# Gathered rows and heads' outputs turned by transposing DMAs on SP's queue instead of by TensorE and ScalarE

## The chip, the cores and the metric

The kernel runs on one core of a Trainium2 chip. Its time is the device time of one execution in microseconds; lower is better. Engines are called as in the profile: PE (TensorE), DVE (VectorE), ACT (ScalarE), POOL (GpSimd) and SP (SyncE, which here only issues DMAs).

## The reference

Eight sequences of 1024 tokens with 512 features are normalised to xn. The result is x plus a Mamba-2 block of xn plus a routed attention of xn. The change concerns the attention. In it, each of 4 groups ranks the tokens by router logits, takes 512 of them as queries and 256 as keys and values, and attends with 8 heads of 64 features:

```python
q_top, q_idx = jax.lax.top_k(jnp.einsum('bnd,gd->bgn', x, w_qr), 512)
queries = x[bidx, q_idx]
kv_top, kv_idx = jax.lax.top_k(jnp.einsum('bnd,gd->bgn', x, w_kvr), 256)
key_values = x[bidx, kv_idx]
q = jnp.einsum('bgnd,ged->bgne', queries, w_q)
k, v = jnp.split(jnp.einsum('bgnd,ged->bgne', key_values, w_kv), 2, axis=-1)
# heads; v *= sigmoid(kv_top); one null key and value in front
attn = jax.nn.softmax(jnp.einsum('bghid,bghjd->bghij', q, k) * DH ** -0.5, axis=-1)
o = jnp.einsum('bghij,bghjd->bghid', attn, v)            # heads side by side: (b, g, 512, 512)
o = jnp.einsum('bgne,gde->bgnd', o, w_out) * jax.nn.sigmoid(q_top)[..., None]
# scatter-add to the tokens, mean over how often each was taken, null token where never
```

## The kernel before, in words

The first half of the program (to about 1856 us) is the Mamba block; it also writes every normalised token to DRAM (`rows`) as two half-precision parts, high and low, so that products come close to single precision (three matmuls for each: high by high, high by low, low by high). The second half is the attention, 32 items (4 groups by 8 sequences). An item n is made of steps:

- DVE finds the tokens' places from their ranks (`rank`, L1803, from `rbc`, which SP loads in two parts, `rank_load`, L2417) and writes them as indices (`slot`). POOL gathers six blocks of 128 rows by indirect DMAs into `gat[0]` to `gat[5]` (`gather`, L2270): four of queries, two of keys.
- `row(n, j)`: a block has one token per partition, but the projections need features on partitions. PE turns the 8 squares of 128 x 128 of a block into a PSUM bank (L1332), ACT copies them to `xq` (queries) or `xk` (keys) (L2116).
- PE projects: `q` (L1345, 4 steps of 12 matmuls), `k` (L1360, 2), `v` (L1374, 2). ACT takes the high part of each, DVE the low part. SP copies halves of `ka` (`keys`, L2423) and `qa` to `qb` (`q_again`, L2429).
- `max` (L1390, 16 steps) and a reduction give each query's maximum; this shift is turned and SP puts it into `qb` (`shift_in`, L2435). The scores (L1420, L1421) wait for it.
- For each of 8 heads: `score` on PE, exponential to `pf` (L2153) and high part to `ph` (L2159) on ACT, low parts on DVE (L1901) and POOL (L2297), `value` on PE (L1437 to L1441), the division on DVE (L1910), then `o_high` on ACT (L2164) and `o_low` on POOL (L2302), which fill `ohl`, the outputs of all heads.
- `oturn(n, qt)`: PE turns the 8 squares of one block of 128 queries from `ohl` (L1449), ACT copies them to `oT[qt]` (L2171).
- `out(n, qt)`: 12 matmuls (L1460) give the output block; ACT scales it (`res`, L2178), POOL adds it to the result in DRAM by an indirect DMA (`store`, L2291).

The items overlap: while the heads of item n run, PE also prepares item n + 1, and turns and projects the outputs of item n - 1. What stands where is decided when the program is built: `make_plan` mixes PE's steps by shares (`Part(feed, start, end)`), and an `Order` then plays all engines through with a duration for each step and lays every engine's instructions down in the order in which they would start. `add(engine, us, step, after, seats, extra)` gives a step its duration, what it comes after, its PSUM banks, and `extra`, how long after its end its result lands. On the chip each engine works its list off in order; semaphores make it wait. `Queue.wait_ge` leaves out a wait that an earlier one covers.

The Mamba block already has two kinds of transposing DMAs on SP: `turn` (L2346, tile `xhT` from `xh`, 128 x 1024 halves) and `gate` (L2352, `yT` from `yhl`, 128 x 2048).

Of the kernel before, what the change touches and what calls it, by code (L numbers as in the profile page):

```python
# [12 lines left out]
P = 128  # L13
# [36 lines left out]
NSLOT = 4  # L50
NW = 4 * D
# [313 lines left out]
def chain(*gens):  # L365
# [10 lines left out]
    "row": [("single", 1, 1.2)],  # L376
# [8 lines left out]
    "oturn": [("single", 1, 1.4)],  # L385
# [5 lines left out]
    "row": [(0.6, "row_out")],  # L391
# [8 lines left out]
    "oturn": [(0.6, "oturn_out")],  # L400
# [9 lines left out]
    "row": lambda n, j: (("gather", n, j), 4.0),  # L410
# [5 lines left out]
    "oturn": lambda n, qt: (("o_low", n, H - 1), 0.8),  # L416
    "out": lambda n, qt: (("oturn_out", n, qt), 0.6),
# [20 lines left out]
def arrange(plan, line):  # L438

    first = [("x_in", 0)]  # L440
    alone = Order(plan.twin(), first, ahead=AHEAD_M)
    arrange_steps(alone, [step for step in line if step[0] not in ("rank_in", "slots", "row")], False)
    alone.run()
    order = Order(plan, first, [t for step, t in alone.at.items() if alone.nodes[step][0] == "DVE"], ("bit", "ranks", "ranks_zero"), ahead=AHEAD_M)
    arrange_steps(order, line, True)
    order.run()


def arrange_steps(order, line, late):
# [13 lines left out]
    for step in line:  # L463
# [26 lines left out]
        elif name == "row":  # L490
            add("PE", 0.45, step, [("gather", 0, b)], [("single", [("row_out", 0, b)])])
# [118 lines left out]
    for j in range(RT):  # L610
        add("POOL", 1.05, ("gather", 0, j), [("slot", 0)], extra=3.0)
        add("ACT", 0.6, ("row_out", 0, j), [("row", 0, j), ("z", NCH - 1, 1)])


def arrange_items(plan, line):

    done = [("weight_low", 0, k) for k in range(FIRST_SLICES)] + [("nulls", 0), ("slot", 0)]
    for j in range(RT):
        done += [(name, 0, j) for name in ("rank", "gather", "row", "row_out")]
# [15 lines left out]
    def back_by(name, n, h, k):  # L635
# [3 lines left out]
    seats = {"q": "q_low", "k": "k_low", "v": "v_low", "row": "row_out", "max": "max_out", "shift_turn": "shift_out",  # L639
             "null_turn": "null_out", "score": "soft", "value": "norm_o", "oturn": "oturn_out", "out": "res"}  # L640
    takes = {"q": 2.6, "k": 2.62, "v": 2.6, "row": 0.45, "max": 0.23, "shift_turn": 0.24, "null_turn": 0.24,
             "score": 0.88, "value": 0.95, "oturn": 0.45, "out": 2.6}
    for step in line:
        name, n, k = (*step, 0)[:3]
        if name == "row":
            after = [("gather", n, k)]
        elif name in "qkv":
            after = each("row_out", n, QT if name == "q" else RT) + [("weight_low", n // NB, NSP // 4 * ("qkv".index(name) + 1) - 1)]
# [10 lines left out]
        elif name == "oturn":  # L659
            after = [("o_low", n, H - 1)]  # L660
        else:
            after = [("oturn_out", n, k), ("weight_low", n // NB, NSP - 1)]
# [12 lines left out]
    for n in range(ITEMS):  # L675
        if n:
# [13 lines left out]
        for e in range(KT):  # L690
            add("ACT", 1.2, ("k_out", n, e), [("k", n, e), two] + ([("keys_id", 1)] if n == 1 else []))
            add("DVE", 1.4, ("k_low", n, e), [("k_out", n, e)])
            add("ACT", 0.7, ("v_out", n, e), [("v", n, e), ("row_out", n, RT - 1), ("value", n - 2, H - 1)])
# [15 lines left out]
        for h in range(H):  # L709
# [16 lines left out]
def make_plan():  # L726
# [68 lines left out]
    for j in range(RT):  # L795
        record.append(("row", 0, j))
# [3 lines left out]

    def turn_rows(n):
        for j in range(RT):
            yield ("row", n, j)
            yield 0.43
# [37 lines left out]
    def turn_out(n):  # L842
        for qt in range(QT):
            yield ("oturn", n, qt)
            yield 0.43

# [9 lines left out]
    for gen in (prepare(0), maxima(0), turn_rows(1)):  # L856
        Feed(gen, 1, record).to(1)
    for n in range(ITEMS):
        others = []
        if n:  # L860
            others.append(Part(Feed(turn_out(n - 1), QT * 0.43, record), -2.9, 6.0))
# [1648 lines left out]
```

## Time and profile before

| | |
|---|---|
| median of 3 runs | 3683.78 us (3683.2 to 3689.54) |
| the profiled execution, its own time | 3691.88 us |
| its span, first to last instruction | 3690.6 us |
| PE busy | 3470.4 us, 94% |
| DVE, ACT, POOL busy | 2934.9 (80%), 2445.5 (66%), 1871.1 (51%) |
| granted PE clock, mean | 0.98 |
| DMA packets | 498362, 344.43 MB |

The page cuts the span into 40 slices of 92 us. A digit is the busy share in tenths, PEclk the granted clock, DMA the share of the 16 DMA engines; the attention begins in slice 21:

```profile
PE   6899999999999999999669999999999999999998
DVE  6898988989898988989968767777767777677764
ACT  5767776677676676776346666676666766666665
POOL 1332423333333433333348788776566766566565
PEclk9899999999999999999879999999999999999999
DMA  5454454455454444544374344354333434334333
```

A line of the list of groups reads: line, engine, operation, written tile <- read tiles (buffer numbers left out; `pair` is PSUM, `id` the identity matrix of a transpose), shapes, count | busy us, mean ns of one | idle time of the engine just before, and what ended it. SPq is the queue of DMAs that SP issues; the duration of such a row is the time that SP takes to issue, and "landing" the time from issue until the data have arrived.

### The profile page before, as it was taken

The page shows a single profiled execution, that of the slowest core. Times are in us where ns is not written, and L with a number is a line of the kernel's source. Part 1 is how long each engine was busy: PE and PEld are TensorE (multiplying, and loading weights), DVE is VectorE, ACT ScalarE, POOL GpSimd, SP SyncE. Part 2 cuts the span into 40 slices and gives each one's busy share as a digit, 9 for nine tenths or more (in the row PEclk, how much of TensorE's full clock was granted, in tenths as well). Part 3 has the DMA queues.
Part 4 walks back from the last instruction along what each step waited for, and adds up shares of the span by engine and source line. Part 5 has one row for each costly group of instructions (what it writes and reads, how often), then busy time and mean ns, then how long its engine had stood idle before and what let it go on. Part 6 is the DMA issues. An engine that isn't in the chain of part 4 may idle for free.

```text
span 3690.6 us, 69594 instructions
## 1 busy us (share of the span) xinstructions
PE 3470.4 (94%) x26872; PEld 2075.7 (56%) x26872; DVE 2934.9 (80%) x5336; ACT 2445.5 (66%) x4649; POOL 1871.1 (51%) x1483
## 2 busy tenths in 40 slices
PE   6899999999999999999669999999999999999998
PEld 4455555555555555555335656656666566666665
DVE  6898988989898988989968767777767777677764
ACT  5767776677676676776346666676666766666665
POOL 1332423333333433333348788776566766566565
PEclk9899999999999999999879999999999999999999
DMA  5454454455454444544374344354333434334333
GB/s 158 98 110 109 114 103 86 101 124 121 113 120 92 107 102 109 116 101 92 67 123 84 74 74 80 72 112 86 69 74 80 105 73 83 71 72 83 70 68 39
DMA packets 498362, 344.43 MB, mean 93 GB/s; under 512 B 239368, under 2 KB 422792, under 8 KB 495985
## 3 DMA queue, kind: packets, MB, share of 16 engines
q1 hardware_dynamic: 441712, 237.05, 28.1%
q0 software_dynamic: 56320, 102.94, 16.3%
q8 instruction: 213, 3.49, 0.4%
q14 instruction: 117, 0.95, 0.1%
HBM read 176.19 MB, written 101.71 MB: 75 GB/s over the span
## 4 chain that ended last, share of the span: by engine, by line
PE 69%; DVE 14%; DMA 4%; issue 4%; ACT 3%; POOL 1%; another core or an unknown queue 0%; DVEq 0%; ACTq 0%
PE pair L1345 8%; PE pair L1297 7%; PE pair L1219 7%; PE pair L1460 6%; PE pair L1267 6%; PE pair L1360 4%; PE pair L1307 4%; PE pair L1374 4%; PE pair L1421 3%; PE pair L1420 3%; PE pair L1390 2%; PE pair L1278 2%; PE pair L1287 2%; PE pair L1441 2%; PE pair L1332 2%
## 5 line engine op out<-in xcount | busy, mean ns | idle before, releaser
L2297 POOL TENSOR_TENSOR ph<-pf,ph 128x512 f16<-128x512 f32 x256 | 380.0, 1486 | 317.7 <-ACT ph L2159 314.7
L1610 DVE SCALAR_TENSOR_TENSOR cv<-raw,taps,cv 128x512 f32<-128x512 f32 x480 | 429.0, 921 | 27.8 <-ACT cv L2018 26.5
L1866 DVE TENSOR_REDUCE smx<-pair 128x2 f32<-128x514 f32 x512 | 350.3, 686 | 79.7 <-PE pair L1390 76.5
L1219 PE MATMUL pair<-xhT,whi 128*128 128x512 f16 x1280 | 385.4, 383 | 8.0 <-ACT btok L2038 2.1
L1297 PE MATMUL pair<-ohi,yT 128*128 128x512 f16 x1024 | 322.5, 387 | 39.1 <-DMA yT<-yhl 38.3
L1267 PE MATMUL pair<-zhi,xhT 128*128 128x512 f16 x1024 | 329.8, 384 | 8.5 <-ACT btok L2038 7.5
L2153 ACT ACTIVATE pf<-pair 128x1024 f32<-128x1024 f32 x256 | 262.1, 1024 | 92.3 <-PE pair L1421 88.3
L1901 DVE TENSOR_TENSOR ph<-pf,ph 128x512 f16<-128x512 f32 x256 | 232.0, 907 | 99.7 <-ACT ph L2159 97.4
L2048 ACT ACTIVATE de<-de,cum 128x128 f32<-128x128 f32 x1024 | 309.4, 388 | 1.2
L2159 ACT CAST ph<-pf 128x1024 f16<-128x1024 f32 x256 | 267.9, 1047 | 4.5
L1828 DVE SCALAR_TENSOR_TENSOR qa<-pair,qa 64x512 f16<-64x512 f32 x256 | 176.6, 690 | 92.1 <-ACT qa L2124 88.4
L1307 PEld LDWEIGHTS pair<-xdt,de 128*128 128x128 f32 x2048 | 239.7, 193 | 16.7 <-issue 8.7
L2302 POOL TENSOR_TENSOR ohl<-of,ohl 128x256 f16<-128x256 f32 x256 | 202.2, 799 | 85.8 <-ACT ohl L2164 83.7
L1219 PE MATMUL pair<-xhT,wlo 128*128 128x512 f16 x640 | 244.5, 382 | 0.0
L1307 PE MATMUL pair<-xdt,de 128*128 128x64 f32 x2048 | 237.7, 275 | 3.8 <-DVE dxs L1646 3.8
L2291 POOL DMA_INDIRECT y<-res,slot_i x128 | 213.5, 1668 | 51.6 <-ACT res L2178 31.9
L1441 PE MATMUL pair<-vhi,ph 128*128 128x65 f16 x2048 | 238.4, 194 | 0.0
L1439 PE MATMUL pair<-vhi,ph 128*128 128x65 f16 x2048 | 238.4, 194 | 0.0
L1440 PE MATMUL pair<-vlo,ph 128*128 128x64 f16 x2048 | 237.9, 193 | 0.0
L2231 POOL TENSOR_TENSOR yn<-yn,neghalf 128x1 f32<-128x1 f32 x64 | 48.7, 760 | 350.3 <-DVE yn L1700 350.1
L2270 POOL DMA_INDIRECT gat<-rows,slot_i x192 | 194.0, 1010 | 58.6 <-issue 29.0
L1219 PEld LDWEIGHTS pair<-xhT,whi 128*128 128x128 f16 x1280 | 123.8, 99 | 168.9 <-issue 35.2
(267 smaller groups left out, 10300.2 us busy)
## 6 DMA issues: line engine op xcount, KB each, us to landing
de<-cum SPq DMA_DIRECT2D x64, 1024.0 KB, 9.4
rows<-rowt SPq DMA_DIRECT2D x16, 1040.0 KB, 6.6
xin<-x SPq DMA_DIRECT2D x16, 1024.0 KB, 8.7
y<-xin SPq DMA_DIRECT2D x16, 1024.0 KB, 5.9
y<-ob POOLq DMA_DIRECT2D x64, 256.0 KB, 4.5
qb<-qa SPq DMA_DIRECT2D x32, 512.0 KB
rbc<-rank SPq DMA_DIRECT2D x63, 256.0 KB
wst<-wkv SPq DMA_DIRECT2D x32, 256.0 KB
```

The lines of the kernel that those rows point to most:

```text
L1219: ins = pe.matmul(bk[:], w[:, k, ws], xt[:, ha, k, :], start=n == 0, stop=n == 3 * KD - 1)
L1267: pe.matmul(pz[:], xt[:, ha, k, cs], w[:, k, j * 512:(j + 1) * 512], start=n == 0, stop=False)
L1297: ins = pe.matmul(bk[:], yT[:, ha * KI + k, :], w[:, k, :], start=k == 0 and n == 0, stop=k == KI - 1 and n == 2)
L1307: ins = pe.matmul(pw[:, h * HD:(h + 1) * HD], de[ch % 2][:, h, :], xdt[:, h, :], start=True, stop=True)
L1345: ins = pe.matmul(bk[:], w[:, k, ws], xq[:, ha * KD + k, :], start=n_ == 0, stop=n_ == 3 * KD - 1)
L1441: ins = pe.matmul(o, p_[:, 1, j, qs_], vhi[u][:, j, h, :], start=False, stop=j == KT - 1, skip_group_check=True)
L1610: ve.scalar_tensor_tensor(c_[:], r_[:, t:t + BLK], taps[:, ct, t:t + 1], c_[:], ALU.mult, ALU.add).then_inc(done, 1)
L1866: ve.tensor_reduce(smx[:, qt, 2 * h2:2 * h2 + 2], sc[:, :, 0:NK + 1], AX.X, ALU.max)
L2048: ins = ac.activation(d_[:, h, :], d_[:, h, :], ACT.Relu, bias=cum_t[i % 2][:, c, h:h + 1], scale=-1.0)
L2153: ac.activation(f[:].rearrange("p k q -> p (k q)"), bank("score", n, h)[:], ACT.Exp, scale=SCALE).then_inc(S.pf, 1)
L2159: ac.copy(p_[:, 0], f[:]).then_inc(S.ph, 1)
L2297: po.tensor_tensor(p_[:, 1, 1], f[:, 1], p_[:, 0, 1], ALU.subtract).then_inc(S.plp, 1)
```

## The change

The two kinds of transposes leave PE and their copies leave ACT. SP issues them as transposing DMAs from SBUF to SBUF: one for each gathered block (six an item, `row`), and one for two blocks of outputs (two an item, `oturn(n, a)`). For the latter `ohl` is laid out as query block, high or low, feature, and `oT` becomes two tiles of two blocks. The PSUM seats of both kinds disappear. POOL's next gather into `gat[j]` now waits until all turns of its kind (queries or keys) have landed, ACT's first cast of the next item into `ohl` until both output turns have landed. The scale of v from the gathered keys stays on DVE as a step of its own, `row_score`. The planner gets durations for the new steps, and the shares by which PE's steps are mixed are set anew; some tiles change places in SBUF.

```diff
+ROW_ISSUE, ROW_LANDS = 0.6, 4.0
+O_ISSUE, O_LANDS = 0.6, 5.0
...
-    "out": lambda n, qt: (("oturn_out", n, qt), 0.6),
+    "out": lambda n, qt: (("oturn", n, qt // 2), 4.0),
...
-                add("POOL", 1.05, ("gather", n, j), [("slot", n), ("row", n - 1, j), ("row_out", n - 1, j)], extra=4.0)
-                add("ACT", 0.6, ("row_out", n, j), [("row", n, j), ("q", n - 1, KD - 1) if j < QT else ("v_low", n - 1, KT - 1)])
+                add("POOL", 1.05, ("gather", n, j), [("slot", n), ("row", n - 1, RT - 1 if j >= QT else QT - 1)] + ([("row_score", n - 1, j)] if j >= QT else []), extra=4.0)
+                read = ("q", n - 1, KD - 1) if j < QT else ("v", n - 1, KT - 1)
+                add("SP", ROW_ISSUE, ("row", n, j), [("gather", n, j), read], extra=ROW_LANDS)
...
-            add("ACT", 0.42, ("o_high", n, h), [("norm_o", n, h)] + each("oturn", n - 1, QT))
+            add("ACT", 0.42, ("o_high", n, h), [("norm_o", n, h)] + each("oturn", n - 1, QT // 2))
...
-            add("ACT", 0.6, ("oturn_out", n, qt), [("oturn", n, qt), ("out", n - 1, qt)])
+            if qt % 2 == 0:
+                add("SP", O_ISSUE, ("oturn", n, qt // 2), [("o_low", n, H - 1), ("out", n - 1, qt + 1)], extra=O_LANDS)
...
-    for gen in (prepare(0), maxima(0), turn_rows(1)):
+    for gen in (prepare(0), maxima(0)):
...
-            others.append(Part(Feed(turn_out(n - 1), QT * 0.43, record), -2.9, 6.0))
...
-            others.append(Part(Feed(maxima(n + 1), 10.2, record), -0.6, 1.1))
+            others.append(Part(Feed(maxima(n + 1), 10.2, record), -0.7, 1.1))
...
-            others.append(Part(Feed(finish(n - 1), 10.4, record), -1.0, 1.0))
-        if n + 2 < ITEMS:
-            others.append(Part(Feed(turn_rows(n + 2), RT * 0.43, record), -1.9, 1.25))
+            others.append(Part(Feed(finish(n - 1), 10.4, record), -0.7, 1.2))
...
-            def row(n, j):
-                g16 = gat[j][:].bitcast(F16)
-                q.wait_ge(S.gat[j], 16 * (n + 1))
-                wait_given_back(q, "row", n, j)
-                b16 = bank("row", n, j)[:].bitcast(F16)
-                for c in range(2 * KD):
-                    ins = pe.transpose(b16[:, c * P:(c + 1) * P], g16[:, c * P:(c + 1) * P], id16[:])
-                ins.then_inc(S.gt_mm, 1)
...
             def norm_o(n, h):
                 q.wait_ge(S.of, H * n + h + 1)
-                q.wait_ge(S.oT_mm, QT * n)
-                ac.copy(ohl[:, 0, :, h * DH:(h + 1) * DH], of[h % 2][:]).then_inc(S.oh, 1)
...
+                for a in range(2):
+                    q.wait_ge(S.oT[a], 16 * n)
+                ac.copy(ohl[:, :, 0, h * DH:(h + 1) * DH], of[h % 2][:]).then_inc(S.oh, 1)
...
             def gather(n, j):
                 q.wait_ge(S.slot, n + 1)
-                q.wait_ge(S.gt_mm, RT * (n - 1) + j + 1)
+                q.wait_ge(S.xr[j // QT], 16 * (KT if j // QT else QT) * n)
...
+            def row(n, j):
+                q.wait_ge(S.gat[j], 16 * (n + 1))
+                if n == 0:
+                    q.wait_ge(S.z_mm, 2 * NCH)
+                    q.wait_ge(S.xs, NCT * NBLK)
+                if j < QT:
+                    q.wait_ge(S.q_mm, KD * n)
+                else:
+                    q.wait_ge(S.k_mm, KT * n)
+                    q.wait_ge(S.v_mm, KT * n)
+                dst, s0 = (xq, j) if j < QT else (xk, j - QT)
+                sp.dma_start_transpose(dst[:, :, s0 * P:(s0 + 1) * P], gat[j][:].bitcast(F16)[:, 0:2 * D]).then_inc(S.xr[j // QT], 16)
...
+            def oturn(n, a):
+                q.wait_ge(S.olo, H * (n + 1))
+                q.wait_ge(S.out_mm, QT * (n - 1) + 2 * a + 2)
+                sp.dma_start_transpose(oT[a][:], ohl[:, 2 * a:2 * a + 2].rearrange("p q h d -> p (q h d)")).then_inc(S.oT[a], 16)
```

SP's instructions for one item in the middle of attention, before. `rbc` is the load of ranks, `qb<-shT` the shift that the scores wait for, `qb<-qa` and `ka<-ka` the copies within one item; in brackets the semaphores that SP waits for.

```order
L2435 DMA qb1<-shT 8x8x512 [waits shiftT]
L2429 DMA qb0<-qa0 64x4096 [waits score_mm,q_high]
L2423 DMA ka0<-ka0 64x8x256 [waits k_high]
L2417 DMA rbc<-rank 128x1024 [waits ranked,slot]
L2417 DMA rbc<-rank 128x1024 [waits ranked]
```

The same stretch after the change, from one output turn to the copy of ka (the second `rbc` follows it):

```order
L2394 DMA_TRANSPOSE oT0<-ohl 128x16x128 [waits out_mm,o_low]
L2371 DMA_TRANSPOSE xq<-gat0 128x8x128 [waits q_mm,gat_in0]
L2394 DMA_TRANSPOSE oT1<-ohl 128x16x128 [waits out_mm]
L2371 DMA_TRANSPOSE xq<-gat1 128x8x128 [waits gat_in1]
L2358 DMA rbc<-rank 128x1024 [waits ranked]
L2371 DMA_TRANSPOSE xq<-gat2 128x8x128 [waits gat_in2]
L2371 DMA_TRANSPOSE xq<-gat3 128x8x128 [waits gat_in3]
L2371 DMA_TRANSPOSE xk<-gat4 128x8x128 [waits v_mm,k_mm,gat_in4]
L2371 DMA_TRANSPOSE xk<-gat5 128x8x128 [waits gat_in5]
L2389 DMA qb1<-shT 8x8x512 [waits shiftT]
L2383 DMA qb0<-qa0 64x4096 [waits score_mm,q_high]
L2377 DMA ka0<-ka0 64x8x256 [waits k_high]
```

The eight turns have moved in between the copies: the second output turn stands behind the first row turn, and the shift behind all six.

ACT's instructions around the turned outputs, before: `vhi` is the high part of v, `oT` the copies of turned outputs, `ohl<-of` the cast of a head's output, `res` the scaling of an output block.

```order
L2140 ACTIVATE vhi<-pair,kscore 128x8x64 [waits row_score,v_mm]
L2171 COPY oT<-pair 128x512 [waits o_turned] x3
L2164 CAST ohl<-of 128x4x64 [waits o_turned,o_head]
L2171 COPY oT<-pair 128x512
L2140 ACTIVATE vhi<-pair,kscore 128x8x64 [waits v_mm]
L2153 ACTIVATE pf<-pair 128x1024 [waits p_low_p,p_low_v,score_mm]
```

After:

```order
L2087 ACTIVATE vhi<-pair,kscore 128x8x64 [waits row_score,v_mm]
L2087 ACTIVATE vhi<-pair,kscore 128x8x64 [waits v_mm]
L2100 ACTIVATE pf<-pair 128x1024 [waits p_low_p,p_low_v,score_mm]
L2106 CAST ph<-pf 128x1024 [waits value_mm,p]
L2119 ACTIVATE res<-pair,qsc 128x512 [waits score_in0,res_out0,out_mm]
L2112 CAST ohl<-of 128x4x64 [waits oT1,oT0,o_head]
```

The first cast of the next item now stands behind the softmax step and behind the `res` of the first output block, and waits for both turns.

## Rows read from the trace of the kernel before

**Rows 1.** Stretches: length, PE, PEld, DVE, ACT, POOL busy (instructions), PEclk, DMA share, GB/s.
```profile
1900.00:2300.00 400.00, 373.13 (x3689) 233.70 (x3689) 302.36 (x681) 256.49 (x391) 322.33 (x270) 0.98 0.43 86
...
2386.80:3599.00 1212.20, 1186.14 (x11891) 747.92 (x11889) 881.65 (x2031) 809.34 (x1223) 781.19 (x688) 1.00 0.40 80
```

**Rows 2.** Waits of PE, 1900 to 3650 us: total us, times, longest.
```profile
PE pair L1437 <- ACT xq L2116: 6.9, 20, 0.8
```

**Rows 3.** Groups of instructions by line: busy us, mean ns, idle before.
```profile
L1332 PE MATMUL pair<-id,gat 128*128 128x128 f16 x1536 | 111.0, 223 | 32.9 <-DMA gat<-rows,slot_i 24.1 <-DVE snl L1867 4.6 <-ACT res L2178 1.8
...
L1449 PE MATMUL pair<-id,ohl 128*128 128x128 f16 x1024 | 68.9, 222 | 2.3 <-POOL ohl L2302 2.3
```

**Rows 4.** The chain of waits, 2600 to 2640 us: start, length, what.
```profile
2609.53 0.89 PE pair L1449 x16
...
2616.95 2.59 PE pair L1460 x12
...
2624.75 0.89 PE pair L1332 x16
...
2633.87 4.36 DMA gat<-rows,slot_i
```

**Rows 5.** Stretch of attention, ACT line 2116 alone, then ACT line 2171 alone.
```profile
1860.00:3690.00 1830.00, 108.90 (x192) 0.99 0.41 80
...
1860.00:3690.00 1830.00, 71.43 (x128) 0.99 0.41 80
```

**Rows 6.** Timeline of SP's queue: start, duration, instruction.
```profile
2639.25 0.76 SPq L2435 DMA_DIRECT2D qb<-shT  x1
...
2660.31 0.61 SPq L2423 DMA_DIRECT2D ka<-ka  x1
...
2715.85 0.61 SPq L2423 DMA_DIRECT2D ka<-ka  x1
```

**Rows 7.** Tiles xhT, then yT: issue in ns min/median/max; landing.
```profile
L2346 SPq DMA_TRANSPOSE xhT<-xh x64: 1232/1291/6160, 32.3 to 1610.4; - x64
...
DMA to landing us min/median/max: 2.7/3.8/10.6
...
L2352 SPq DMA_TRANSPOSE yT<-yhl x64: 1322/1888/3949, 132.1 to 1834.1; - x64
...
DMA to landing us min/median/max: 4.2/4.3/10.4
```

**Rows 8.** Stretches behind a yT turn issued at 1567.73: PEclk, DMA share, GB/s.
```profile
1568.70:1569.70 1.00, 1.00 0.82 162
1569.70:1570.70 1.00, 1.00 1.16 215
1570.70:1571.70 1.00, 1.00 0.79 148
```

**Rows 9.** Timeline of PE where attention begins.
```profile
1869.36 5.45 PE L1332 MATMUL pair<-id,gat 128*128 128x128 f16 x48 [22.19 <-DMA gat<-rows,slot_i]
...
1874.60 0.71 PE L1345 MATMUL pair<-xq,wqhi 128*128 128x512 f16 x2
```

**Rows 10.** Stretches there: PE busy, PEclk, DMA share, GB/s.
```profile
1873.00:1874.00 1.00, 1.00 (x12) 0.50 0.85 243
...
1875.00:1876.00 1.00, 1.00 (x6) 1.00 0.02 4
```

**Rows 11.** Timeline of PE at the last item's end.
```profile
3669.93 3.59 PE L1449 MATMUL pair<-id,ohl 128*128 128x128 f16 x32 [2.31 <-POOL ohl L2302]
...
3673.32 0.54 PE L1460 MATMUL pair<-whi,oT 128*128 128x512 f16 x1
```

**Rows 12.** Timeline of one item, from its last head to its output matmuls.
```profile
2605.04 0.38 PE L1420 MATMUL pair<-qa,ka 128*128 128x512 f16 x1
...
2606.27 0.96 POOL L2270 DMA_INDIRECT gat<-rows,slot_i  x1 [0.33 <-DVE slot_i L1813]
2607.51 0.67 POOL L2302 TENSOR_TENSOR ohl<-of,ohl 128x256 f16<-128x256 f32 x1 [0.28 <-ACT ohl L2164]
```

More of the change, by code:

```diff
@@ L441, in arrange @@
     alone = Order(plan.twin(), first, ahead=AHEAD_M)
-    arrange_steps(alone, [step for step in line if step[0] not in ("rank_in", "slots", "row")], False)
+    arrange_steps(alone, [step for step in line if step[0] not in ("rank_in", "slots")], False)
     alone.run()
@@ L611, in arrange_steps @@
         add("POOL", 1.05, ("gather", 0, j), [("slot", 0)], extra=3.0)
-        add("ACT", 0.6, ("row_out", 0, j), [("row", 0, j), ("z", NCH - 1, 1)])
+        add("SP", ROW_ISSUE, ("row", 0, j), [("gather", 0, j), ("z", NCH - 1, 1)], extra=ROW_LANDS)
+        if j >= QT:
+            add("DVE", 0.1, ("row_score", 0, j), [("gather", 0, j)])
 def arrange_items(plan, line):
@@ L618, in arrange_items @@
     for j in range(RT):
-        done += [(name, 0, j) for name in ("rank", "gather", "row", "row_out")]
+        done += [(name, 0, j) for name in ("rank", "gather", "row")]
+        if j >= QT:
+            done.append(("row_score", 0, j))
     order = Order(plan, done, keep=KEEP, ahead=AHEAD)
@@ L637, in back_by @@
         return (name, *divmod(H * n + h - k, H))
[L639 to L642, printed above, removed]
+    seats = {"q": "q_low", "k": "k_low", "v": "v_low", "max": "max_out", "shift_turn": "shift_out",
+             "null_turn": "null_out", "score": "soft", "value": "norm_o", "out": "res"}
+    takes = {"q": 2.6, "k": 2.62, "v": 2.6, "max": 0.23, "shift_turn": 0.24, "null_turn": 0.24,
+             "score": 0.88, "value": 0.95, "out": 2.6}
     for step in line:
         name, n, k = (*step, 0)[:3]
[L645 to L648, printed above, removed]
+        if name in "qkv":
+            after = each("row", n, QT if name == "q" else RT) + [("weight_low", n // NB, NSP // 4 * ("qkv".index(name) + 1) - 1)]
         elif name == "max":
@@ L799, in make_plan @@
     plan.append(("mamba_done",))
[L801 to L804, printed above, removed]
     def prepare(n):
@@ L1045, in program @@
         qb = [sb(ctx, "qb0", [P, H, NQ], F16)]
-        oT.append(sb(ctx, "oT2", [P, 2 * KD, P], F16))
+        res = [sb(ctx, "res0", [P, D], F32)]
         gat = sb2(ctx, "gat", [P, ROW], F32, RT)
@@ L1064, in program @@
         null_bc = sb(ctx, "null_bc", [P, D], F32)
-        res = [sb(ctx, "res0", [P, D], F32)]
+        res.append(sb(ctx, "res1", [P, D], F32))
         smx = sb(ctx, "smx", [P, QT, H], F32)
@@ L1442, in value @@
                 ins.then_inc(S.pv, 1)
-            def oturn(n, qt):
-                q.wait_ge(S.olo, H * (n + 1))
-                wait_given_back(q, "oturn", n, qt)
-                b16 = bank("oturn", n, qt)[:].bitcast(F16)
-                for j in range(2 * KD):
-                    ins = pe.transpose(b16[:, j * P:(j + 1) * P], ohl[:, j // KD, qt, (j % KD) * P:(j % KD + 1) * P], id16[:])
-                ins.then_inc(S.oT_mm, 1)
             def out_(n, qt):
@@ L2185, in scalar_engine @@
                     "attention": attention, "weight_high": weight, "table": table_, "keys_id": keys_id,
-                    "row_out": row, "q_out": qs, "k_out": ks, "v_out": vs, "null_p": null_p,
-                    "soft": score, "high_p": high_p, "o_high": norm_o, "oturn_out": oturn, "res": out_}
+                    "q_out": qs, "k_out": ks, "v_out": vs, "null_p": null_p,
+                    "soft": score, "high_p": high_p, "o_high": norm_o, "res": out_}
             for step in plan:
```

90 lines of the change are left out of this document (26 added, 64 removed).

## The prediction

> **What bounds the kernel now.** I read the stretches of the attention stage first, then PE's waits, then the chain of waits through one item, and single timelines where a number was wanted. The change touches attention alone, the second half of the span. In its middle PE is busy 1186.14 of 1212.20 us at full granted clock, DVE 881.65, ACT 809.34, POOL 781.19 [rows 1]: 97.9% against at most 73%. SP issues the same instruction of neighbouring items, the copy inside ka, at 2660.31 and 2715.85 [rows 6]; 22 items fill the stretch, 55 us each, of which PE stands 1.2. Of what it stands, one kind is 6.9 us in 20 pieces and ends with ACT's copies to xq [rows 2], so even that hangs on work that goes. PE's own queue is the bound: what leaves it shortens the span one for one, unless the new route makes PE wait.
>
> **What is removed, and how to size it.** By the groups of lines, the transposes of gathered rows keep PE busy 111.0 us and those of the heads' outputs 68.9 us [rows 3], 179.9 together. That is too much: busy time of a line alone counts the tail of its last matmul, in which the next step's matmuls already run. The chain shows what a step really occupies: 16 transposes, two steps, take 0.89 us for either kind [rows 4], 0.445 us for a step of 8. There are 32 x 6 + 32 x 4 = 320 steps. 310 of them lie inside the run: 310 x 0.445 = -138 us, 4.45 per item of 55. The other ten are the first item's six and the last item's four; they run at the low clock and come below. ACT also loses 108.90 + 71.43 us of copies [rows 5]; it is 67% busy and PE covers all of it, so by itself it is worth nothing. If another engine were the bound, it would be a gain, no cost.
>
> **What is added: per item six turns of rows and two of outputs, all on SP.** The stage before attention has both instructions. The turn of 128 x 1024 halves (256 KB, one gathered block) holds SP 1.29 us and lands after 3.8; the turn of 128 x 2048 (512 KB, two blocks of outputs) holds it 1.89 us and lands after 4.3; the worst landed after 10.6 and 10.4 [rows 7]. SP is held 6 x 1.29 + 2 x 1.89 = 11.5 us more per item of 50; it issues little now, so the queue has room. What matters is what stands behind a waiting turn.
> On the DMA engines, a lone 512 KB turn takes shares of 0.82, 1.16 and 0.79 in three stretches of 1 us [rows 8]: 2.8 us of all sixteen; half of that, 1.4, for 256 KB. Per item 6 x 1.4 + 2 x 2.8 = 14 us, beside 0.40 x 55 = 22 us of today [rows 1]: 36 of 50.5 us, a share of 0.71. That is busy, not full, and landings may grow. The Trainium skill ("Advanced Engine Details and Errata", section X-Bar Transpose (TRN2)) says that transposing DMAs are as fast as regular ones, 350 to 400 GB/s expected; by that, 512 KB take an estimated 1.4 us and the share would be 0.57. The trace does not agree: the lone turn moved at most 215 GB/s in a stretch [rows 8]. I go by the row.
>
> **Outputs.** In the item shown the last head leaves PE at 2605.04 and its low half is made by 2607.51 + 0.67 = 2608.18 [rows 12]; then 4.3 to land, 2612.5. Meanwhile PE has, in the new order, a score, half of v and a head's values (today these end at 2609.53, 4.4 us after 2605.04 [rows 4, 12]), then the other half of v (12 wide matmuls, 2.59 us as in [rows 4]), another score, another head's values and two maxima (4.4 - 2.6 = 1.8, and about 0.4): 9.2 us, until 2614.2. The turn is in time by 1.7 us. ACT's first cast into ohl for the next item now waits for both output turns. The second stands behind a row turn that waits for a gather issued at 2606.27 [rows 12]; a gather takes 4.36 from issue to use [rows 4]: 2610.6, then 1.3 for the row turn's issue and 4.3 to land, 2616.2. In ACT's new order a res stands before that cast, which waits for the first output matmuls, 2614.2 + 2.6 = 2616.8. So this wait is covered by the other.
> **Rows.** The last row turn of an item waits for the last gather, issued at 2633.87 and there 4.36 us later, 2638.2 [rows 4]; with 1.3 us of issue, SP would come to the copy of the shift (qb<-shT) at 2639.5, and it does so at 2639.25 today [rows 6]. Nothing is lost; q and k of the turned rows begin later than that.
> **New waits, in between.** By medians none of the three shows, with margins of 0.6 to 1.7 us against landings that scatter up to 6 us above their median [rows 7]. I take 0.25 us per item, +8 us (bounds 0 and 31 x 6.1 = 189, every output turn at the worst landing). Against it stand waits that go with the steps: 6.9 us [rows 2], and before the row turns 32.9 - 22.2 = 10.7 us [rows 3, 9]. I take half of these 17.6, -9 us (bounds -18 and 0).
>
> **Start.** PE turns from 1869.36 and begins q at 1874.60 [rows 9]. Now SP issues four turns from 1869.4, the last at 1869.4 + 3 x 1.29 = 1873.2, landed at 1877.0: q is 2.4 us later. PE has stood 22.19 us by then [rows 9], and its granted clock is 0.50 (1.2 GHz) while it turns, 1.00 (2.4 GHz) from 1875 on [rows 10]. The turns took the slow stretch, 5.2 us; now q's matmuls do, at half speed, +2.6. Together +5.0.
> **End.** The last outputs are turned from 3669.93, the output matmuls begin at 3673.32 [rows 11], 3.4 us; a DMA takes 4.3, +0.9, and PE comes back from standing, +2.6 by the same reckoning. +3.5.
>
> **Sum.** -138 + 8 - 9 + 5.0 + 3.5 = -130.5 us. The profiled execution took 3691.9 us (its span 3690.6): 3561.4. The median of the runs, 3683.8, is 8.1 us below it: 3553.
>
> **Rivals.**
> A (10%), the full busy time counts and waits vanish: -179.9 for all 320 steps, with 5.0 + 5.2 and 3.5 + 3.4 given back at the ends: -163, 3521 (3510 to 3530). For it: the groups' busy time [rows 3]. Against it: 0.89 us for 16 in the chain [rows 4].
> B (17%), turns hidden in part: the landings grow with the DMA share from 0.40 to 0.71 by 3 us, 1.3 us more than the outputs' margin, and the ACT cast is late as well; 1.3 to 3 us per item, +40 to +93: 3593 to 3646. For it: single landings of 10 us. Against it: the medians are from shares of 0.4 to 0.5 too.
> C (5%), slower: SP issues the second output turn behind the row turn that waits for gather 0. If gathers, under the added traffic, take 9 us more than 4.36, that turn lands at 2625 and ACT stands at its ohl cast for 8.5 us; scores are not drained and PE stands. 31 x 8.5 = 263 us: 3816. It decides from 130.5 / 31 = 4.2 us per item on. Against it: gathers are spread over 28 us of the item, and ordinary ones go between the turns' packets. The Trainium skill ("VectorE: DVE Perf Modes", sections The three transpose paths and Rules for kernel authors) is on the side of B and C: TensorE turns 128 x 128 in 390 ns, the DMA crossbar in 1309, and TensorE is to be used where PSUM will do. For one turn the trace agrees (3.8 us to land 8 blocks [rows 7], 0.445 on PE [rows 4]); the rule prices latency, and here PE's time is what is short.
> D (4%), POOL bounds the first items, where it also makes weights: busy 322.33 of 400 us [rows 1], 87% if 7 items lose 4.45 us each. If it gives back half of them, +16: 3569, inside my range.
> E (2%), waits of 4 us per item eat it all: no change.
>
> **How the numbers follow.** My forecast, 3535 to 3585, 62%. The range, 3520 to 3600, adds D, most of A and the lower edge of B. About 0.2%, 7 us, is what a measurement of this kernel can tell from no change: faster 0.93, same 0.02, slower 0.05.
>
> **What would show each step.** Items of about 51 us at SP's copy of ka; PE's share in the middle of attention still 97% or more; no wait of PE for DMA xq or xk after the first item, and little for oT; row turns landing in about 4 us, output turns in 4.3 to 5; a DMA share of 0.7; q 2.4 us later behind the first gathers, at the low clock. I am wrong if one of PE's waits for a turn passes 1 us per item, or if ACT stands at its first ohl cast.

## The result: 34 us faster, where 130 were forecast

| | before | changed | |
|---|---|---|---|
| median of the runs, us | 3683.8 | 3649.4 | ratio 0.990, 95% interval 0.988 to 0.992 |
| profiled execution, us | 3691.9 | 3642.1 | its span: 3690.6, 3640.7 |

The change makes the kernel 1.0% faster; 3553 us was forecast, from 3520 to 3600. The profiled executions are 49.8 us apart; the sum, made between profiled executions, was 130.5. So 81 us are missing (96 by the medians, which are 34 us apart; the profiled execution of the changed kernel is the fastest of its four). The page of the changed kernel (its span in 40 equal slices, and SP's queue with its packets, MB and share of the 16 DMA engines):

```profile
PE   6899999999999999999748999999999999999997
...
PEclk9899999999999999999868999999999999999998
DMA  5444544465554445444387576777676676577664
...
q1 hardware_dynamic: 777584, 320.97, 42.5%
```

The DMA row holds 6 and 7 where it held 3 and 4; this came as forecast (0.71). The stretches of attention show what did not. First the changed kernel, then the kernel before over the same long stretch (columns as in [rows 1]):

```profile
1900.00:2300.00 400.00, 358.49 (x3163) 207.25 (x3164) 303.96 (x678) 220.96 (x320) 318.96 (x267) 0.94 0.70 131
...
1900.00:3500.00 1600.00, 1501.40 (x13602) 881.71 (x13603) 1235.54 (x2767) 932.96 (x1356) 1109.29 (x983) 0.97 0.70 132
```

```profile
1900.00:3500.00 1600.00, 1546.15 (x15427) 973.20 (x15428) 1178.24 (x2691) 1057.61 (x1602) 1107.31 (x959) 1.00 0.41 82
```

PE stands for 1600 - 1501.4 = 98.6 us where it stood for 53.9, and its granted clock is 0.97 where it was 1.00. Summed over the 80 stretches of 20 us in it (20 us times 1 less the clock), the clock takes 43.0 us; before, 6.8. So 45 us went into idle time of PE and 36 into its clock, 81 together, about what is missing. This is an account of one stretch and not an exact sum: a low clock while PE stands costs nothing but is counted in the 36, and the first and last items lie outside the stretch.

Single items show the same. An item is taken from one copy inside ka on SP to the next. The first row below is an item of the kernel before; the second is an item of the changed kernel without a long wait, the third one with waits:

```profile
3381.10:3435.70 54.60, 54.12 (x545) 34.16 (x544) 39.16 (x93) 35.68 (x53) 34.18 (x31) 1.00 0.38 75
```

```profile
3286.10:3335.90 49.80, 49.39 (x466) 29.74 (x465) 39.42 (x92) 29.84 (x44) 31.89 (x30) 1.00 0.70 132
3069.60:3129.90 60.30, 55.07 (x466) 31.02 (x464) 41.96 (x99) 30.49 (x43) 32.97 (x32) 0.92 0.62 120
```

With the same 466 matmuls an item takes 49.8 or 60.3 us. In the good one PE's work is 4.73 us less than before (forecast 4.45); five items have 49.8, while the mean of the 31 distances between these copies is (3544.76 - 1887.00) / 31 = 53.5, before 55.1. Of the 10.5 us between the two, 5.7 are more busy time for the same matmuls, at a mean clock of 0.92. The loss is not spread evenly: the first seven distances sum to 379.6 us and before to 375.8, no gain at all, where 31 us was forecast; the other 24 are 53 us shorter, of 107.

What begins the bad item is in its chain of waits (start, length, what):

```profile
3071.48 0.68 POOL ohl L2243
3072.17 7.88 DMA oT<-ohl
3080.05 0.05 issue
3080.10 4.45 PE pair L1421 x12
...
3085.22 2.59 PE pair L1421 x12
3087.81 0.22 PE pair L1359 x2
```

The last half of ohl is written at 3072.16, the turn is issued at once and lands 7.9 us later, not 4.3. PE has done what the order put in between and stands 1.8 us. The 12 output matmuls behind it take 4.45 us, and 2.59 a little later: the wait cost 1.8 us and the clock as much again. Stretches of 2 us show the clock:

```profile
3076.00:3078.00 2.00, 2.00 (x34) 1.46 (x33) 1.86 (x5) 1.47 (x2) 0.00 (x0) 1.00 1.26 263
3078.00:3080.00 2.00, 0.27 (x9) 0.15 (x5) 1.97 (x6) 1.28 (x2) 0.60 (x1) 1.00 0.52 197
3080.00:3082.00 2.00, 1.90 (x5) 0.73 (x6) 1.90 (x3) 0.00 (x0) 0.55 (x1) 0.54 0.88 162
3082.00:3084.00 2.00, 2.00 (x7) 0.74 (x6) 0.00 (x0) 0.00 (x0) 0.00 (x0) 0.61 1.14 211
3084.00:3086.00 2.00, 2.00 (x14) 1.20 (x13) 1.19 (x3) 0.98 (x2) 0.45 (x1) 1.00 0.80 151
```

The DMA engines are full in the 2 us before PE stands (share 1.26), not while it stands (0.52). In the two stretches behind the idle time the clock is 0.54 and 0.61, near the lower level (1.2 GHz). The Trainium skill ("TensorE: Matmul & The Clock Gate", Part 1) says that the chip sets this clock by how busy TensorE has been of late; the rows agree.

SP's timeline of this item has the queue that the prediction spoke of: the second output turn is issued 8.2 us after the first, behind the row turn that the prediction expected to wait for its gather.

```profile
3072.17 3.65 SPq L2394 DMA_TRANSPOSE oT<-ohl  x1
3079.10 1.24 SPq L2371 DMA_TRANSPOSE xq<-gat  x1
3080.39 1.81 SPq L2394 DMA_TRANSPOSE oT<-ohl  x1
```

PE's longest waits of the changed kernel from 1900 to 3540 us, and one of ACT's from 1900 to 3550 (total us, times, longest):

```profile
PE pair L1421 <- DMA oT<-ohl: 16.1, 11, 3.8
PE pair L1359 <- DVE snl L1827: 13.8, 17, 2.8
PE pair L1359 <- DVE of L1870: 8.9, 5, 2.2
PE pair L1367 <- DVE shift L1832: 7.6, 2, 5.3
```

```profile
ACT ohl L2112 <- DMA oT<-ohl: 40.7, 26, 4.3
```

Only the first names a DMA. The next three are steps of the maxima, which wait for VectorE: for reductions and the shift made of them (`snl`, `shift`), and for the division of a head's output (`of`). The kernel before already had waits of this kind, and [rows 2] shows only the fourth line of its list. The three above it, 1900 to 3650 us, were as large or larger and belong to steps that stay:

```profile
PE pair L1406 <- DVE pnm L1890: 10.5, 8, 2.9
PE pair L1390 <- DVE snl L1867: 9.0, 11, 2.1
PE pair L1420 <- DVE snl L1867: 7.9, 6, 1.8
```

ACT's stand at its ohl cast is what I had named as a sign of being wrong. From this reading I held the output turns guilty, with the clock that their waits take; the first experiments test that.

### The profile page after: what moved, and what is told of

It reads as the page before. It is cut to its first block, busy times and chain, and to the rows that moved or that the text cites. A ratio compares the mean times of both kernels' runs of the same rounds, so it can differ in the third digit from the quotient of the medians.

```text
span 3640.7 us, 64398 instructions
## 1 busy us (share of the span) xinstructions
PE 3360.3 (92%) x24312; PEld 1940.5 (53%) x24312; DVE 2962.7 (81%) x5336; ACT 2273.6 (62%) x4329; POOL 1850.6 (51%) x1483
## 4 chain that ended last, share of the span: by engine, by line
PE 58%; DVE 14%; DMA 8%; issue 5%; POOL 5%; ACT 4%; SPq 1%; another core or an unknown queue 0%; POOLq 0%; ACTq 0%; DVEq 0%
PE pair L1314 7%; PE pair L1275 7%; PE pair L1197 7%; PE pair L1421 7%; PE pair L1245 6%; PE pair L1285 4%; PE pair L1329 3%; DMA oT<-ohl 2%; PE pair L1343 2%; PE pair L1389 2%; PE pair L1390 2%; PE pair L1359 2%; PE pair L1256 2%; PE pair L1265 2%; DMA de<-cum 2%
## 5 line engine op out<-in xcount | busy, mean ns | idle before, releaser
L2238 POOL TENSOR_TENSOR ph<-pf,ph 128x512 f16<-128x512 f32 x256 | 354.8, 1386 | 243.8 <-ACT ph L2106 241.6
L1861 DVE TENSOR_TENSOR ph<-pf,ph 128x512 f16<-128x512 f32 x256 | 254.8, 995 | 84.3 <-ACT ph L2106 81.3
L1285 PEld LDWEIGHTS pair<-xdt,de 128*128 128x128 f32 x2048 | 244.7, 196 | 20.4 <-issue 12.5
L1408 PE MATMUL pair<-vhi,ph 128*128 128x65 f16 x2048 | 243.8, 196 | 0.5 <-issue 0.5
L1410 PE MATMUL pair<-vhi,ph 128*128 128x65 f16 x2048 | 243.7, 195 | 0.3 <-issue 0.3
L1406 PE MATMUL pair<-nvb,pnT 96*128 96x65 f16 x1024 | 202.3, 198 | 21.3 <-issue 6.7
```

The costliest lines, as they stand in the source:

```text
L1285: ins = pe.matmul(pw[:, h * HD:(h + 1) * HD], de[ch % 2][:, h, :], xdt[:, h, :], start=True, stop=True)
L2238: po.tensor_tensor(p_[:, 1, 1], f[:, 1], p_[:, 0, 1], ALU.subtract).then_inc(S.plp, 1)
```

## The experiments

Medians in us; each ratio is to the kernel before, run beside it on the same chip. The median of the kernel before was 3681 to 3691 there, so kernels that did not run beside each other are compared by their ratios (0.001 is 3.7 us). An interval of a ratio is some 8 us to either side. PE idle, the sum of the clock's loss (as above) and the DMA share are of the 1600 us from 1900 on in the profiled execution. Each kernel named _weave has an order of its own, described below, so a difference between two of them also holds how well each order came out.

| kernel | median | ratio (95%) | PE idle | clock | DMA |
|---|---|---|---|---|---|
| before | 3684 | 1 | 54 | 7 | 0.41 |
| changed | 3649.4 | 0.990 (0.988 to 0.992) | 99 | 43 | 0.70 |
| rows_only | 3690.5 | 1.000 (0.999 to 1.002) | 99 | 40 | 0.58 |
| outs_only | 3648.6 | 0.988 (0.986 to 0.991) | 58 | 16 | 0.52 |
| planner_costs | 3643.2 | 0.987 (0.984 to 0.989) | 98 | 46 | 0.70 |
| before_weave | 3656.7 | 0.993 (0.990 to 0.995) | 28 | 6 | 0.41 |
| outs_weave | 3597.3 | 0.976 (0.974 to 0.978) | 21 | 7 | 0.54 |
| rows_weave | 3631.3 | 0.987 (0.984 to 0.990) | 59 | 19 | 0.62 |
| both_weave | 3620.2 | 0.984 (0.981 to 0.987) | 87 | 39 | 0.74 |
| keys_weave | 3611.0 | 0.979 (0.977 to 0.981) | 40 | 10 | 0.60 |
| outs_shadow | 3631.9 | 0.984 (0.981 to 0.986) | 42 | 17 | 0.71 |
| outs_small | 3605.0 | 0.979 (0.977 to 0.981) | 23 | 8 | 0.56 |
| outs_stall | 3782.0 | 1.025 (1.022 to 1.027) | 120 | 75 | 0.49 |

### One half of the change at a time

rows_only puts the outputs' steps back on TensorE and ScalarE, outs_only the rows'. The core of each edit to the changed kernel:

```diff
 rows_only, TensorE:
+            def oturn(n, qt):
+                q.wait_ge(S.olo, H * (n + 1))
+                wait_given_back(q, "oturn", n, qt)
+                ... ins = pe.transpose(b16[:, j * P:(j + 1) * P], ohl[:, qt, j // KD, ...], id16[:])
 outs_only, TensorE:
+            def row(n, j):
+                q.wait_ge(S.gat[j], 16 * (n + 1))
+                wait_given_back(q, "row", n, j)
+                ... ins = pe.transpose(b16[:, c * P:(c + 1) * P], g16[:, c * P:(c + 1) * P], id16[:])
```

> Only the gathered rows are turned by transposing DMAs (192 of them); the heads' outputs go back to TensorE and ScalarE (128 steps), with the weave of the kernel before for them. Theory: what ate the forecast gain is the output turns alone: they land some 7 us after their issue in the loaded queue, PE waits for oT, and the short idle times lower the granted clock. Then this kernel removes 192 x 0.445 = 85 us of PE and pays nearly nothing: 3600 to 3620 us, below the changed kernel (3649), clock 0.99 and over from 1900 to 3540, DMA share about 0.57. Rival 1 (every transposing DMA costs in proportion to its bytes, through a loaded DMA side: slower gathers, clock, DVE): a gain in proportion, 0.6 x 34 us, so about 3664 us. Rival 2 (the written order is what costs, not the transfers): PE idles in front of the max and score steps as this planner's order has it, 3640 or more, with no wait for a DMA among the first.

Measured: 3690.5, no gain. My theory is wrong as it stood: the row turns alone take 85 us of work off PE and give nothing. It came out as rival 2 had it. PE idle and clock lose as much as in the changed kernel, 99 and 40 us.

> Only the heads' outputs are turned by transposing DMAs (64 of them, 512 KB each); the rows are turned on TensorE and ScalarE as before. Theory: output turns are the cost: 128 x 0.445 = 57 us of PE removed, some 25 us of waits for oT and some 20 us of clock given back: 3665 to 3690 us, with oT still landing over 6 us after its issue and the clock below 0.99. Rival 1 (load in proportion to bytes): 3670 us too, but with oT landing in about 5 us, since the rows' turns are gone from the queue, and waits for oT under 10 us. If the turns cost only what was forecast (landing 4.3 us): 3630 us.

Measured: 3648.6, as much as the whole change, and better than the theory and rival 1 had it. PE waits 5.1 us for oT. The output turns are not the guilty half: alone they gain as much as both kinds together.

planner_costs tells the planner what the trace shows, which alters the order of instructions only:

```diff
-ROW_ISSUE, ROW_LANDS = 0.6, 4.0
-O_ISSUE, O_LANDS = 0.6, 5.0
+ROW_ISSUE, ROW_LANDS = 1.3, 4.0
+O_ISSUE, O_LANDS = 3.0, 4.5
```

> The changed kernel with the planner told what its trace shows: a row turn takes SP 1.3 us and lands 4.0 us later, an output turn takes SP 3.0 us and lands 4.5 us later (before 0.6 + 4.0 and 0.6 + 5.0). Only the order of the instructions changes. Theory: PE's waits for oT (22.7 us) shrink, since out comes later in the order, and a part of the clock comes back: 3615 to 3640 us. Rival (the loss is contention and does not hang on order): within 5 us of 3649.

Measured: 3643.2, its interval overlaps the changed kernel's. The theory's detail came true and its sum did not: PE waits 0.4 us for oT, and stands as long as before. PE's first waits are now in the maxima:

```profile
PE pair L1359 <- DVE snl L1827: 20.5, 32, 2.4
PE pair L1359 <- ACT pf L2100: 12.9, 15, 0.9
...
PE pair L1421 <- DMA oT<-ohl: 0.4, 1, 0.4
```

rows_only has the same picture, without one DMA among its first waits:

```profile
PE pair L1388 <- DVE pnm L1871: 22.4, 16, 3.2
PE pair L1372 <- DVE snl L1848: 19.3, 30, 2.7
PE pair L1372 <- ACT pf L2121: 16.3, 29, 0.9
PE pair L1402 <- DVE snl L1848: 14.2, 18, 2.9
```

New theory O: the turns were filler, short work that PE had while the maxima waited. A maxima step gives PE 0.22 us of matmuls (the last row of the chain above) for a pair of banks that VectorE then reduces in two pieces, 512 in all; by the groups of the changed kernel (busy us, mean ns):

```profile
L1826 DVE TENSOR_REDUCE smx<-pair 128x2 f32<-128x514 f32 x512 | 349.7, 684 | 88.3 <-PE pair L1359 85.5 <-issue 2.0
```

0.22 us on PE, 2 x 0.68 on VectorE. By the theory the turns stood in between; take them out, and PE stands there, unless other work is put in.

### The order set anew, with and without turns

In four kernels the shares between which the weave spreads each kind of step were chosen again. both_weave against the changed kernel (with planner_costs' lines, and 6.0 us for a gather's landing in place of 4.0):

```diff
-KEEP = 4.0
-AHEAD, AHEAD_M = 12, 4
+KEEP = 8.0
+AHEAD, AHEAD_M = 16, 4
-            others.append(Part(Feed(prepare(n + 1), 20.8, record), 0.2, 2.0))
-            others.append(Part(Feed(maxima(n + 1), 10.2, record), -0.7, 1.1))
+            others.append(Part(Feed(prepare(n + 1), 20.8, record), -0.2, 1.9))
+            others.append(Part(Feed(maxima(n + 1), 10.2, record), -0.6, 1.0))
-            others.append(Part(Feed(finish(n - 1), 10.4, record), -0.7, 1.2))
+            others.append(Part(Feed(finish(n - 1), 10.4, record), -1.1, 1.8))
```

> The control: the kernel before, no turn moved, only its weave set anew in the same way (prepare 0.1 to 1.8, maxima -0.5 to 1.1, finish -1.1 to 1.9, row turns -2.5 to 1.75, output turns -1.9 to 7.2). Its PE was busy for 97 to 99% of each stretch. Theory O: at most 0.5% faster, 3670 to 3690 us, so that what the other three win belongs to the turns. If it gains 1% or more, the new order is worth its gain without any transposing DMA and the moved turns are worth less than the comparison says.

The control, 3656.7, more than I expected of it: the order alone is worth 0.7%, so the others are compared with it. Its PE stands 28 us of 1600 instead of 54.

> Outputs by transposing DMAs, rows on TensorE (as outs_only, 3648.6 us), with the measured costs of an output turn and the weave set anew (prepare 0.0 to 2.1, maxima -0.9 to 1.1, finish -1.5 to 2.0, row turns -1.5 to 1.55). Its PE was idle for 58.5 us of 1640, near the 54.4 us of the kernel before, so theory O and rival D both leave little to win: 3630 to 3650 us.

3597.3, far below what I expected, 59.4 us under the control (128 x 0.445 = 57; the difference is known to some 11 us), and the fastest kernel here. PE stands 21 us of 1600:

```profile
1900.00:3500.00 1600.00, 1578.58 (x15464) 983.38 (x15463) 1278.05 (x2825) 1042.71 (x1576) 1131.51 (x1007) 1.00 0.54 104
```

> Rows by transposing DMAs, outputs on TensorE (as rows_only, 3690.5 us, the time of the kernel before), with the weave set anew (prepare 0.5 to 1.4, maxima -0.4 to 1.1, finish -0.8 to 1.6, output turns -2.2 to 6.3, 20 steps of leeway). Theory O: the 85 us of TensorE work that the row turns took then come back, less some 20: 3610 to 3640 us. Rival D: whatever the order, row turns by DMA give nothing: 3675 or more, PE idle about 100 us of 1640.

3631.3: 25 us under the control, of the 85 that the steps took. By the ratios the new order brought 49 us here (1.000 to 0.987) and 27 in the kernel before, so 22 us more than without the change. It did not bring the rest of the 85 us. PE waits 21.7 us for turned rows here, 1900 to 3500 us, against 5.3 in the changed kernel.

```profile
PE pair L1327 <- DMA xq<-gat: 21.7, 11, 2.9
```

> The changed kernel in another order: the planner is told the measured costs of the turns (SP 1.3 us and 4.0 us for rows, 3.0 and 4.5 for outputs) and of a gather (6.0 us to land instead of 4.0), and the weave of attention's steps is set anew (prepare from -0.2 to 1.9, maxima -0.6 to 1.0, finish -1.1 to 1.8, 8 us and 16 steps of leeway). Nothing is computed otherwise. Theory O (order): the removed turns were the work that PE did while the maxima waited for their reductions on VectorE; with other work put there, PE's idle time from 1900 to 3540 falls from 101 us to 60 or less, and the clock with it above 0.985: 3590 to 3620 us. Rival D (load of the DMA side): PE's idle time and clock stay, 3640 to 3650 us.

3620.2: order gives the changed kernel 0.6%, less than expected, and no more than it gave the kernel before (0.7%). Against the control the full change gains 36.5 us, against the kernel before it gained 34. So theory O fits each half alone (the new order brings the outputs 45 us and the rows 49, where the control has 27) and not the two together: PE stands 87 us of 1600 and the control 28. An order that would serve both is not ruled out. The kernel stays 23 us above outs_weave although its PE has 2.67 us less to do per item, 85 us in all; 108 us are to be explained. Of the long stretch:

```profile
1900.00:3500.00 1600.00, 1513.45 (x13832) 897.04 (x13833) 1260.18 (x2805) 942.91 (x1371) 1138.73 (x1000) 0.98 0.74 134
```

The copies inside ka say where this lies. In the first eleven of the 31 distances both_weave is 26.6 us slower than outs_weave (595.5 and 569.0; 18.4 of it in the first), and in the other twenty 9.6 us faster (1040.9 and 1050.6). PE is busy 91% of the first part at a clock of 0.95, and 96% of the second at 0.99, while the DMA share is 0.74 in both. GpSimd is busy 80% of the first part and 66% of the second.

Two things differ from outs_weave on the DMA side. Gathers land in 6.6 us at the median, 4.0 in outs_weave (tile gat, both_weave first):

```profile
DMA to landing us min/median/max: 4.0/6.6/10.5
```

```profile
DMA to landing us min/median/max: 3.2/4.0/11.5
```

The share alone does not set this landing: it is 4.7 us in before_weave at a share of 0.41 and 3.9 in rows_weave at 0.62, and rows_weave still lacks 60 of its 85 us. And SP stands in front of row turns for gathers, 437.1 us in 111 pieces, with all that is queued behind:

```profile
SPq L2371 <- DMA gat<-rows,slot_i: 437.1, 111, 9.4
```

### Load or queue

outs_shadow adds the load of the row turns to outs_weave, 256 KB each from a weight tile into a tile that nobody reads. Room for it comes from four tiles that only pad, so other tiles change places. The next weights wait until the copies out of their tile have landed:

```diff
+            def shadow(n, j):
+                if n < 2:
+                    return
+                ...
+                q.wait_ge(S.gt_mm, RT * n + j + 1)
+                q.wait_ge(S.shadow, 16 * (RT * (n - 2) + j))
+                sp.dma_start_transpose(spare[:], src).then_inc(S.shadow, 16)
```

> outs_weave (3597.3 us; outputs by transposing DMAs, rows on TensorE and ScalarE) with the load of the row turns added and nothing else: from item 2 on SP issues, when TensorE has turned a block of rows, one transposing DMA of 256 KB from a weight tile into a tile that nobody reads (180 in all). PE does all its work as before, no step waits for these copies. Theory C (the DMA side is loaded, so all that lives on it comes late): the loss by which both turns in DMAs (3620) stand above outs_weave comes back here, 3612 us or more, with gathers landing in over 6 us (4.0 in outs_weave) and PE idle 60 us or more of 1600. Theory L (the latency of a turned row and what SP queues behind its wait for a gather is what costs, not the load): at most 8 us more, 3597 to 3605, PE idle under 35 us.

3631.9, 28 us by the ratios (0.0076 x 3684), with no step of attention waiting for the copies. That is as much as the 23 us between both_weave and outs_weave, as theory C said; but PE stands 42 us and not 60, and how fast the gathers land can't be read in this trace. The equality is not the whole comparison either: both_weave has 85 us less work, so the added copies account for 28 of its 108 us. What a turned row costs by its latency, and by what SP holds back for a gather, is not cleared. The loss lies early here too: 19.3 us in the first eleven distances, 3.8 in the other twenty, 6.2 already before the first copy inside ka and so before any copy of the shadow. SP also stands in the new waits (189 us for PE, 326 for the copies). Hence the same with 32 KB each:

```diff
-                sp.dma_start_transpose(spare[:], src).then_inc(S.shadow, 16)
+                sp.dma_start_transpose(spare[:, 0, :], src).then_inc(S.shadow, 16)
```

> outs_shadow (3631.9 us) with the same 180 additional transposing DMAs at the same places and with the same waits of SP, but of 128x128 values (32 KB) in place of 256 KB, to an unused tile. outs_shadow lost 28 us against outs_weave (ratios to the kernel before 0.9836 and 0.9760). Theory C (the load of the DMA engines is what costs): the loss goes with the bytes, ratio 0.976 to 0.979, gathers land in about 4 us again. Rival Q (SP's queue is what costs: it stands still for a turn's wait, and what is queued behind it is late): the loss stays, ratio 0.981 to 0.985. Half and half: about 0.980.

Ratio 0.979, between the two. 17 of the 28 us go with the bytes (0.9836 against 0.9790, the intervals just apart); the other 11, SP's queue, are not clearly told from nothing (0.977 to 0.981 against 0.974 to 0.978; the two profiled executions, 3600.9 and 3601.2, are alike). Gathers land in 4.8 us.

keys_weave moves only the two key blocks of an item to DMAs, beside the outputs:

> Between outs_weave (3597.3) and both_weave (3620.2): outputs and the two blocks of key rows by transposing DMAs (64 steps less on TensorE, 28 us), the four blocks of query rows on TensorE; weave set anew for it. If the loss with the turned rows grows with every turn moved, 3600 to 3615 us. If it begins only where the DMA side is over some 0.65 busy, a gain of half the 28 us or more: 3575 to 3590 us, the best so far.

3611.0, not below outs_weave: of the 28 us that 64 steps free, nothing is left, at a DMA share of 0.60. The gain that a limit at 0.65 would have given did not come. By the profiled executions the last twenty distances are 12.5 us shorter than those of outs_weave and the first eleven 15.6 longer, the split of both_weave again.

### What a wait of TensorE costs

outs_weave with one wait more, behind an item's last value step:

```diff
                 ins.then_inc(S.pv, 1)
+                if h == H - 1:
+                    q.wait_ge(S.olo, H * (n + 1))
```

> outs_weave with one wait more per item: after the last value step of an item TensorE waits until GpSimd has written the low half of that head's output. Same work, same DMAs. TensorE was idle for 21 us of 1600 at a clock deficit of 7 us. The new wait is 2 to 4 us long, so 60 to 110 us of idle time in all. Theory K (waits of TensorE lower the granted clock after them): the time grows by the waits and by 30 to 60 us of clock on top, and the clock stands at 0.96 to 0.98 from 1900 to 3500: 3690 to 3750 us. Rival (the clock fell from the DMA load or by itself): it stays at 0.99 to 1.00, 3660 to 3700 us.

3782.0, more than either side expected. The new wait is 96.2 us in 27 pieces:

```profile
PE pair L1354 <- POOL ohl L2283: 96.2, 27, 5.1
```

Idle time grew by 99 us of 1600, the clock's loss by 68, with a DMA share below outs_weave's. So theory K: the waits lower the clock, at no change in the work, by 0.7 us for each us of idle time. The whole execution gives a little less: the profiled ones are 176 us apart, and 31 waits at this mean take 110, which leaves 66 us, 0.6 for each. One of these waits in stretches of 2 us:

```profile
3094.00:3096.00 2.00, 0.29 (x10) 0.17 (x6) 1.64 (x4) 2.00 (x3) 0.88 (x1) 1.00 0.99 199
3096.00:3098.00 2.00, 0.54 (x3) 0.42 (x4) 0.00 (x0) 1.20 (x2) 2.00 (x3) 0.53 0.93 322
3098.00:3100.00 2.00, 2.00 (x12) 1.39 (x11) 1.36 (x3) 0.00 (x0) 1.48 (x2) 0.50 0.77 148
3100.00:3102.00 2.00, 2.00 (x11) 1.45 (x10) 0.13 (x1) 0.00 (x0) 0.00 (x0) 0.50 0.94 173
3102.00:3104.00 2.00, 2.00 (x16) 1.61 (x15) 0.00 (x0) 1.19 (x2) 0.00 (x0) 0.77 0.20 81
```

## Why the prediction was wrong, step by step

- **What bounds the kernel** held: PE did. The sentence drawn from it, that what leaves PE's queue shortens the span one for one, held for the output turns (59 of 57 us, outs_weave against before_weave) and not for the rows (25 of 85 alone; beside the outputs 23 us lost).
- **The size of a step**, 0.445 us, held: an item without waits has 4.73 us less of PE's work, 4.45 forecast. Rival A, the full busy time, would be 5.6 and is out.
- **DMA share** 0.71: 0.70. **Row turns** are issued in 1.3 us and PE of the changed kernel hardly waits for them. The output turn is not what was forecast: 3.0 us of SP at the median, 1.89 taken from [rows 7]:

```profile
L2371 SPq DMA_TRANSPOSE xq<-gat x123: 1231/1302/3152, 1900.4 to 3516.0; - x123
...
L2394 SPq DMA_TRANSPOSE oT<-ohl x60: 1613/2998/4913, 1992.7 to 3549.1; - x60
```

- **The margin of 1.7 us for the outputs** failed: where an output turn stood on the chain between 2000 and 3500 us it took from 6.1 to 10.6 us, against 4.3. Those are the late ones; the median of all is 5.9 in both_weave and 5.5 in outs_weave, at shares of 0.74 and 0.54. So the median of [rows 7], from another stage, was too low for attention at either load. PE's waits for oT were 16 us of its 99, and planner_costs took them away for 6 us of gain, its interval overlapping the changed kernel's.
- **New waits, in between** is the step that failed: 0.25 us per item stood for 45 us / 30 = 1.5 of idle time and 36 / 30 = 1.2 of clock that went with it. It asked about three waits for turned data (with margins of 0.6 to 1.7 us, but the third, 2639.5 against 2639.25, had none) and, on the other side, took 9 us off for waits that would vanish; it left out the larger waits of PE for VectorE in the maxima, which the trace of the kernel before had. It didn't ask what PE does there once the turns are gone, nor what the added load does. What the runs show of these two: a new order is worth 22 us more in rows_only than in the kernel before, and in the changed kernel nothing more; added copies cost up to 28 us, 17 of them by their bytes. Neither accounts for the whole loss, and its cause stays open for the rows.
- **The end**: from the last copy inside ka to the end of the span it took 3690.6 - 3598.9 = 91.7 us and takes 3640.7 - 3544.8 = 95.9; +4.2 for +3.5. This stretch holds more than the last turns. **The start** cost less than the +5.0. The first gather is issued at 1849.83 and q begins at 1868.20, 18.4 us later; before it was 1855.94 and 1874.60, 18.7. So q is not 2.4 us later behind its gathers. Its matmuls do begin at the low clock. From the first gather to the first copy inside ka it is 37.2 us instead of 35.8, +1.4.
- **Rival B** was the nearest in its number, 3593 to 3646, but partly by luck: late output turns explain the smaller part of the idle time, and it had no term for the clock. **C**'s queue exists (the second output turn behind the row turn that waits for a gather; ACT stands 40.7 us), but costs ACT 1.6 us at a time and not 8.5. **D** had the right place, the first items, and not shown the right engine: outs_weave keeps PE busy 392 of the 400 us from 1900 with GpSimd at 342, the changed kernel 358 with 319.

Left open: what makes up the 108 us between both_weave and what outs_weave less the row steps would give. Added copies account for 28 of them at most; the latency of a turned row, SP's wait for gathers and the order were not told apart. Bytes alone don't separate the two kinds either: both free the same per byte (57 us for 64 turns of 512 KB, 85 for 192 of 256 KB). Nor was it settled why the loss lies in the first eleven items, at the same DMA share as later. Turning the rows by DMAs only in the later items would test that, and a row turn issued with nothing queued behind it would test SP's part; neither was tried.

## What to carry to other kernels

Work that leaves a full engine is worth its time only if the engine does not come to stand in its place. Look at which short steps stood around it and what those wait for, and set the order anew before judging the change, with a control that gets a new order too (here the same row turns came out at 0.0% and 1.3%, the same output turns at 1.2% and 2.4%, where the order alone was worth 0.7). Test the halves of a change alone: one of these two was worth its full time, and the other took back a part of it. A median landing time read in one stage is no margin in another. In this kernel a wait of TensorE of some us cost 1.6 to 1.7 times its length, for the clock behind it.

## What the runs showed of the hardware

- A wait of 1.8 us halved the granted clock (0.54 and 0.61 in the two stretches of 2 us behind it); over 27 waits of 3.6 us (outs_stall) the clock cost 0.6 to 0.7 us for each us of idle time.
- The issue of a 512 KB transposing DMA held SP 1.89 us at the median in the first stage and 3.0 in attention of the changed kernel, 4.9 at most. The mean DMA share does not order these times: in attention they are 3.5 us in outs_stall at 0.49, 3.8 in outs_weave at 0.54, 3.0 in the changed kernel at 0.70. What does is open. The Trainium skill ("Advanced Engine Details and Errata", X-Bar Transpose (TRN2)) expects 350 to 400 GB/s of transposing DMAs; the lone turn moved 215 in its best stretch [rows 8], and with that the DMA engines were full.
- VectorE's subtraction for ph (128x512), which the change does not touch, took 907 ns at the mean before, 995 after and 1036 in outs_weave, whose GpSimd stands less (209.6 us in front of its own such step, 317.7 before). That stand is not the cause by itself: in outs_shadow it is 212.6 us, and the subtraction takes 895 ns. I have not told the cause apart.
